# A pair loop of causal attention written in cycles of four steps instead of two, with batch jobs two at a time in every second cycle

## The reference

```python
x = x + attn_a(layernorm(x), ...)      # softmax(q k^T / 4 + bias, causal) v, then Wo
x = x + ffn(layernorm(x), ...)
x = x + attn_b(layernorm(x), ...)      # rotary q, k; the same softmax
x = x + ffn(layernorm(x), ...)
```

## Time and profile before

| what | value |
|---|---|
| median of 3 runs | 4371.92 us (4366.13 to 4383.42) |
| span of the profiled execution | 4403.8 us |
| PE busy | 4131.5 us (94%) |
| DVE busy | 2924.1 us (66%) |
| ACT busy | 2789.4 us (63%) |
| mean granted clock of PE | 0.970 of full |

### The profile page before, as it was taken

The page is one execution under the profiler, slowest core; times in us unless marked ns, Lnnn a source line. Parts: engine busy times, 40 slices in busy tenths (PEclk is TensorE's granted clock), DMA queues, the critical chain, the costliest instruction groups (busy, mean ns, idle before and its releaser), DMA issues.

```text
span 4403.8 us, 107634 instructions
## 1 busy us (share of the span) xinstructions
PE 4131.5 (94%) x42369; PEld 2542.9 (58%) x42369; DVE 2924.1 (66%) x3987; ACT 2789.4 (63%) x5907; POOL 816.1 (19%) x832
## 2 busy tenths in 40 slices
PE   5799999999999999998989999999999999998875
PEld 4455555555555555557855555555556555554764
DVE  3777787778776887771057778777887688773000
ACT  2377777777777776673247777777777777666211
POOL 3010001110121023410013330333023310110012
PEclk9799999999999999999989999999999999999988
DMA  5223223422333333335533432333333322221553
GB/s 168 46 70 75 51 51 81 106 75 53 86 84 84 71 97 102 100 80 174 179 85 97 121 93 51 106 103 98 63 98 95 97 68 59 61 67 50 165 170 117
DMA packets 247473, 407.02 MB, mean 92 GB/s; under 512 B 29324, under 2 KB 162188, under 8 KB 233868
## 3 DMA queue, kind: packets, MB, share of 16 engines
q1 hardware_dynamic: 243896, 391.76, 33.4%
q0 software_dynamic: 3072, 8.39, 0.6%
HBM read 264.25 MB, written 121.50 MB: 88 GB/s over the span
## 4 chain that ended last, share of the span: by engine, by line
PE 81%; DVE 5%; ACT 4%; issue 4%; DMA 3%; SPq 1%; POOL 1%; another core or an unknown queue 0%; ACTq 0%; POOLq 0%; DVEq 0%
PE ps_acc L874 23%; PE ps_r L817 22%; PE ps_p L842 11%; PE ps_r L911 5%; PE ps_r L958 5%; PE ps_p L947 4%; DVE part_max L1074 4%; ACT probs L710 4%; PE ps_r L915 3%; PE ps_r L825 3%; PE ps_r L919 2%; PE ps_p L850 1%; DMA hid_f<-rows_by_expert 1%; PE ps_r L905 1%; PE ps_r L922 1%
## 5 line engine op out<-in xcount | busy, mean ns | idle before, releaser
L1074 DVE TENSOR_REDUCE part_max<-ps_p 128x2 f32<-128x1024 f32 (+3 forms) x2560 | 2599.6, 1060 | 806.6 <-PE ps_p L842 489.0
L710 ACT ACTIVATE probs<-ps_r 128x512 f32<-128x512 f32 (+1 forms) x4608 | 2291.7, 578 | 458.3 <-PE ps_r L817 199.7
L817 PE MATMUL ps_r<-q_stack,k_stack 54*128 54x512 f32 (+3 forms) x5120 | 1647.9, 440 | 61.0 <-issue 16.5
L842 PE MATMUL ps_p<-k_stack,q_stack 52*128 52x512 f32 (+3 forms) x5120 | 1150.8, 407 | 56.9 <-DVE part_max L1074 31.7
L817 PEld LDWEIGHTS ps_r<-q_stack,k_stack 54*128 54x128 f32 x5120 | 721.8, 186 | 784.2 <-ACT probs L710 524.3
L874 PE MATMUL ps_acc<-probs,v_head 128*17 128x256 f32 x19456 | 1156.7, 362 | 2.4 <-ACT acc_sb L718 1.2
L874 PEld LDWEIGHTS ps_acc<-probs,v_head 128*17 128x17 f32 x19456 | 491.3, 97 | 412.0 <-ACT probs L710 135.5
L842 PEld LDWEIGHTS ps_p<-k_stack,q_stack 52*128 52x128 f32 x5120 | 595.4, 189 | 134.9 <-DVE part_max L1074 95.1
L1150 DVE COPY xf<-ps_r 128x256 f32<-128x256 f32 x60 | 25.5, 425 | 459.2 <-PE ps_r L958 459.2
L825 PE MATMUL ps_r<-id,mk 64*128 64x64 bf16 x4096 | 306.6, 195 | 0.0
L911 PE MATMUL ps_r<-xT,wqkv 128*128 128x256 f32 x1024 | 269.1, 397 | 1.9 <-ACT xT L727 1.9
(11 more groups left out here) (90 smaller groups left out, 2094.8 us busy)
## 6 DMA issues: line engine op xcount, KB each, us to landing
probs<-w_dram SPq DMA_DIRECT2D x60, 1024.0 KB, 8.4
q_stack<-parts SPq DMA_DIRECT2D x384, 128.0 KB
k_stack<-parts SPq DMA_DIRECT2D x384, 128.0 KB
parts<-pa SPq DMA_DIRECT2D x128, 256.0 KB, 2.4
parts<-pb SPq DMA_DIRECT2D x128, 256.0 KB, 3.0
o_sums<-acc_sb SPq DMA_DIRECT2D x1024, 17.0 KB
bk<-o_sums SPq DMA_DIRECT2D x64, 256.0 KB
bk<-recips SPq DMA_DIRECT2D x64, 256.0 KB
```

The costliest lines, as they stand in the source:

```text
L710: act.activation(probs[:, at % PBUF, u, 0:w], block_bank(g, n, u)[:, 0:w], ACT.Exp)\
L817: mm[u] = pe.matmul(block_bank(g, n, u)[:, col:col + QW - q0], ks[s][r, kb * P:(kb + 1) * P], qs[s][r, qt * QW + q0:(qt + 1) * QW], start= ...
L842: mm[u] = pe.matmul(banks[:, u, col:col + w], qs[s][r, qb * P:(qb + 1) * P], ks[s][r, kc * QW:kc * QW + w], start=i == 0, stop=True, skip_ ...
L1074: mm = dve.tensor_reduce(part_max[:, :, qb, kc], ps_p[:, p1_banks(g, n), col:col + w], AX_X, ALU.max)
```

## The change

The loop over two steps becomes a loop over four (`CYCLE = 4`), nine cycles for a pair. In a cycle the four units, the eight single-head blocks of scores, and two slots for `times_v` are placed in a new order, which the rows below show. The ring is ordered accordingly, with the jobs of a cycle behind the first block of scores. The units and scores that follow `times_v` (and, in cycles with jobs, the unit behind the jobs) issue their mask products ahead of their score products. `times_v` of a group goes to the first slot at which its steps are done (`value_slots`).

Batch jobs lie in the first, third, fifth ... cycle of a batch, two in each (`slot_step(k) = 8 * (k // 2)`, 72 slots in a batch of 72 cycles). `xt` now turns two row tiles at once, with four products in place of two and one copy of 512 columns. The `c` transposes go to steps 4 and 28. The reciprocal of the softmax sums is done in two halves.

```diff
+CYCLE = 4
+def value_slots():
+    ready = [CYCLE * c + half for c in range(CYCLES + 1) for half in range(2)]
+    ...
-C_HI, C_LO = 30, 6
-JOB_STEPS = (2, 10, 16, 20, 24, 28, 34)
+C_HI, C_LO = 28, 4
+Y_SLOTS = (8, 13, 18, 23, 28, 33, 38, 43, 48, 57, 59, 61, 66, 68, 69, 70)
+def slot_step(k):
+    return 2 * CYCLE * (k // 2)
...
+            def score(g, n, u, masks_first=False):
...
-                for n in range(0, STEPS, 2):
-                    score(g, n, (0, 1))
-                    if g + 1 < NG:
-                        unit(g + 1, n)
-                    score(g, n + 1, (0,))
-                    if g + 1 < NG:
-                        unit(g + 1, n + 1)
-                    score(g, n + 1, (1,))
-                    if n in GROUP_AT:
-                        times_v(g, GROUP_AT[n])
-                    elif n == 0 and g % (NG // 2):
-                        times_v(g - 1, GROUPS - 1)
+                for n in range(0, STEPS, CYCLE):
+                    turned = any(j[0] in RING_JOBS for j in JOBS[g][n])
+                    unit(g + 1, n)
+                    score(g, n, 0)
                     for j in JOBS[g][n]:
                         job(*j)
+                    unit(g + 1, n + 1, masks_first=turned)
+                    score(g, n, 1)
+                    score(g, n + 1, 0)
+                    unit(g + 1, n + 2)
+                    score(g, n + 1, 1)
+                    value_slot(g, n // 2)
+                    unit(g + 1, n + 3, masks_first=True)
+                    score(g, n + 2, 0)
+                    score(g, n + 2, 1)
+                    score(g, n + 3, 0)
+                    value_slot(g, n // 2 + 1)
+                    score(g, n + 3, 1, masks_first=True)
...
                 if kind == "xt":
                     for k in range(KD):
-                        mm = pe.transpose(to[:, k * P:(k + 1) * P], xl[:, i, k * P:(k + 1) * P], identf[:, :])
+                        for t in range(2):
+                            mm = pe.transpose(to[:, k * D + t * P:k * D + (t + 1) * P],
+                                              xl[:, 2 * i + t, k * P:(k + 1) * P], identf[:, :])
```

More of the change, by code:

```diff
@@ L116, in batch_jobs @@
     r = beta - 1 if beta > 0 else None
-    out, loaded, xt_from = [], 0, 22
-    if r is not None:
[L119 to L137, removed]
+    out = []
@@ new lines, in rows @@
+    def rows(f, c, t):
+        return [(t, ("ld", f, c, 0))] + [(t + 7 + 2 * i, ("ln", f, c, i)) for i in range(len(NORM_FROM))]
+    if beta < 0:
+        out += rows(0, 0, -40)
+    if f is not None:
+        at = [slot_step(k) for k in F_SLOTS]
+        for c in range(NQ):
+            x0, x1, at = at[0], at[1], at[2:]
+            nxt = (f, c + 1) if c + 1 < NQ else (f + 1, 0)
+            if nxt[0] < NB:
+                out += rows(nxt[0], nxt[1], x1 + 2)
+            out += [(x0, ("xt", f, c, 0)), (x1, ("xt", f, c, 1)), (x1 + 3, ("cs", f, c, 0))]
+            for kind, u in TURN[c]:
+                if kind == "v":
+                    out += [(at[0], ("v", f, c, u))]
+                    at = at[1:]
+                else:
+                    q1 = at[1]
+                    out += [(at[0], ("qk", f, c, 2 * u)), (q1, ("qk", f, c, 2 * u + 1)),
+                            (q1 + 2, ("sw", f, c, u)), (q1 + 3, ("sp", f, c, u)), (q1 + 10, ("st", f, c, u))]
+                    at = at[2:]
@@ L142, in batch_jobs @@
[L142 to L145, removed]
-    return out
+                out += [(y_at[i], ("y", r, c, i)), (y_at[i] + 2, ("ba", r, c, i))]
+            if routed(r, c):
+                out += [(done + i, ("fn", r, c, i)) for i in range(len(NORM_FROM))]
+            out += [(done + 1, ("bs", r, c, 0))]
+    return out
@@ L777, in _ @@
             for g in range(NG):
-                for n in range(0, STEPS, 2):
+                for n in range(0, STEPS, CYCLE):
                     exp_block(g, n, 0)
+                    for j in JOBS[g][n]:
+                        job(*j)
                     exp_block(g, n, 1)
@@ L802, in _ @@
             mm.then_inc(bias_mm, 1)
-            def score(g, n, heads):
+            def score(g, n, u, masks_first=False):
                 s = g % SLOTS
@@ L830, in unit @@
-            def unit(g, n):
+                pe.wait_ge(ring_used, PLACE[("s", g, n, u)] - RING + 1)
+                bank = block_bank(g, n, u)
+                r, half = slice(HALF * u, HALF * u + ROWS), slice(HALF * u, HALF * u + HALF)
+                masks = [col + HALF * part for qt, kb, q0, col in STEP[n] if kb >= 4 * qt for part in range(2)]
+                fresh = True
+                for part, lo in enumerate(masks if masks_first else ()):
+                    pe.matmul(bank[:, lo:lo + HALF], mk[half, 2 + part % 2, :], id64[half, :], start=fresh, stop=False,
+                              skip_group_check=True)
+                    fresh = False
@@ new lines, in score @@
+                for qt, kb, q0, col in STEP[n]:
+                    mm = pe.matmul(bank[:, col:col + QW - q0], ks[s][r, kb * P:(kb + 1) * P],
+                                   qs[s][r, qt * QW + q0:(qt + 1) * QW], start=fresh, stop=True,
+                                   skip_group_check=True)
+                    fresh = False
+                for part, lo in enumerate(() if masks_first else masks):
+                    mm = pe.matmul(bank[:, lo:lo + HALF], mk[half, 2 + part % 2, :], id64[half, :], start=False,
+                                   stop=True, skip_group_check=True)
@@ L924, in job, with value_slot @@
                 mm.then_inc(job_mm, 1)
+            def value_slot(g, k):
+                if k in GROUP_AT:
+                    times_v(g, GROUP_AT[k])
+                elif k == 0 and g % (NG // 2):
+                    times_v(g - 1, GROUPS - 1)
             def turn_slots(ly, i):
```

132 lines of the change are left out of this document (69 added, 63 removed).

## The result

The changed kernel takes 4525.41 us (median of 4 runs, 4513.57 to 4527.54), the kernel before beside it 4377.67 (median of 4): a ratio of **1.034 [1.032, 1.036]**, slower by 148 us. The forecast was 4400, with a range that ended at 4480. One fact for reading: the profiled execution of the kernel before (4403.8) was some 30 us longer than its median; the one of the changed kernel (4525.0) is its median. So the traces differ by less (121 us) than the medians (148).

What follows compares the result with a forecast made beforehand. Bound: a loop of unit n, reduction, unit n + 2. Cycles + 166 us, jobs - 152, net + 14; side work 20 makes 34, less a few + 28: 4432 profiled, 4400 median; range 4300 to 4480, own 4385 to 4435.

Steps and rivals of the forecast that it cites:

- The loop through unit n, its reduction and unit n + 2: Plain cycle: both units share a bank pair between two `times_v`, PE stands some 0.8 us; cycle 5.63 against 5.30.
- The sign given for it: Profile would show loads of units waiting for `part_max` by 0.7 to 0.9 us once in each plain cycle.
- The side work on DVE: Normalisation parts of 0.65 us behind units n + 1 and n + 3 partly show: 20 us, bounds 0 and 36.
- Loads of scores no longer wait for the scalar engine: New order puts a `times_v` or a unit's wait between each block and its bank's exponential; no wait for `probs`.
- Steps 24 to 27: Unit 24's eight masks and two reductions lengthen the chain to unit 26 by about 0.45 us; cycle + 0.8.
- The five plain ones: Plain cycles of a pair without jobs: + 0.33 us each, less one hidden `c` (0.22), 1.43 together.
- A cycle with jobs: Two jobs lie where PE would wait: 6.83 us against 7.23; a pair 0.73 cheaper, 0.55 on average.
- the rival with a further wait there: Job cycle: second job's bank or reduction n + 1 comes 0.3 us late, adding 75 us: 4475; chance 0.15.
- The price that I gave to the first product behind a change of tile: First load behind a change of tile to the next product of the same array rows: 0.34 us.
- smaller drains: Rival: entries into `times_v` cost 0.22, both cycles 0.2 us shorter, 115 us less: 4285; chance 0.22.
- hidden side work: Rival: side work's 20 us go and masked cycles cost less, 2.3 for 2.6; no change; chance 0.20.
- PE runs through: Rival: unit n + 2 does not wait, plain cycle 4.8 us, kernel near 4110; chance 0.03.

Runs made afterwards that it cites:

- Experiment 2: Changed kernel with unit n + 2 moved behind the first `times_v`, unit n + 3 later, and masks leading in unit n + 2 instead: 4376.61 us, ratio 1.000.
- Experiment 1: Changed kernel with four products of zeros added to each of two score blocks in 240 cycles without jobs and without a `c`: 4450.71 us, ratio 1.017.
- experiment 9: Changed kernel with the normalisation parts moved behind the first unit of cycles with jobs: 4456.49 us, ratio 1.018.
- experiment 11: Kernel before, two-step order, with the batch-job half of the change and normalisation parts moved into cycles with jobs: 4364.18 us, ratio 0.998.
- 5: Kernel before, two-step order kept, with the batch-job half of the change alone: 4439.16 us, ratio 1.016.
- experiment 12: Changed kernel with the zero products of Experiment 1 and the normalisation parts placed as in experiment 9: 4407.21 us, ratio 1.007.
- experiment 7: The order of Experiment 2 with two products of zeros added to each of two score blocks in cycles without jobs: 4377.3 us, ratio 1.001.
- experiment 10: The order of Experiment 2 with the normalisation parts placed as in experiment 9: 4319.48 us, ratio 0.987 to the kernel before.
- experiment 3: Changed kernel with masks last everywhere, all three `masks_first` set to False: 4576.19 us, ratio 1.045.

## Why the prediction was wrong

- **The loop through unit n, its reduction and unit n + 2** was right in place and size: 5.66 for 5.63, DVE's gap 0.91 for 0.8 to 0.9. Experiment 2 moves it out (with unit n + 3 and the order of its masks) and takes off 149 us, the clock's part included. The sign given for it was half wrong: of the wait, the profile puts 0.21 on units and 0.31 on scores.
- **The step that failed is one that was not there: the clock.** I read a PE busy 94% at nearly full granted clock and costed every product at that speed, also in an order into which I had just put a wait of 0.8 in each plain cycle. In that order TensorE falls to 1.2 GHz 58 times for 266 us, mostly in or behind masked cycles, against 9 times for 78. Experiment 1 prices it at 75 us net of the zeros' own time where I had nothing. None of the rivals had it either.
- **The side work on DVE** was named, with bounds of 0 and 36 us and a value of 20. It measures 69 (experiment 9), and 75 in the old order (experiment 11 against 5). The sum took only the part that shows in DVE's own loop. As estimated above, that part is 25 to 31 of the 69 and so within its bounds; the other 38 to 44 are the clock again: with parts in steps 12 to 15 of even pairs it fell there 12 times, without them never, and the low clock could reach into the jobs of the next cycle (pair 14, steps 16 to 19: 8.16 us at clock 0.87, where the median with the full clock is 6.93). Clock and side work overlap: 75 and 69 alone, 118 together (experiment 12; 113 by the difference to the kernel before). That is nearly all of the 120 by which I missed. That experiment 12, at 4407, stands where I had forecast this kernel, at 4400, is in part luck: the 4400 hold 20 for side work, which experiment 12 does without. It is 35 us over the kernel before, where the sum without side work gives 8; another 8 are the zeros' own time, and some 20 are left for what follows.
- **Loads of scores no longer wait for the scalar engine: wrong.** They wait 240 us, down from 524 on the page of before. In plain cycles it is hidden in the reduction's wait. In steps 12 to 15, with one `times_v` in place of two, it isn't (0.53 at 3822.74). That cycle was estimated at 0.2 longer and is 0.7 longer (5.25 against 4.57), the last at 0.1 shorter and is 0.5 longer (5.36 against 4.86). Steps 24 to 27 were overestimated (0.3 for 0.8). The five plain ones come to 1.3 for 1.43. Over a pair without jobs 3.2 for the 2.6 forecast, with the clock left out: 38 us more over 64 pairs.
- **A cycle with jobs**: 6.65 for 6.83. Over the nine kinds of cycle in experiment 12, two jobs add 1.2 on average by medians, 0.7 less than before; I had 0.55. This better half pays for a good part of the worse estimates above. The ring and the second job's bank were not late: the rival with a further wait there falls.
- **Masks first at nothing**: wrong by 51 us, in the kernel's favour (38 at full clock). The price that I gave to the first product behind a change of tile was right for units (0.34), and too high where masks lead.
- Of the rivals, smaller drains and hidden side work are refuted; "PE runs through" too, but experiment 2 comes near its idea: most of the wait on the pair of banks goes if the unit is moved.

Left open: why experiment 7 gained nothing, and why the clock falls in steps 0 to 3 and 16 to 19 and not in plain cycles with a wait as long. That waits bring it down is shown by filling them (experiment 1) and by moving what makes them (2 and 9), not by following one fall.

## What to carry to other kernels

When a change puts waits into a loop that runs at full granted clock, price them twice: by their own length, and by what the next microseconds would cost at half clock; count the stretches at 1.2 GHz in the trace, since the slices of the page hide them. In a chain product, reduction, product that shares a bank pair, let a long foreign stretch of TensorE work (here `times_v`) fall between the two products, and put side work on VectorE where TensorE has other work to do meanwhile. Here the two together made the new order 52 us faster than the old (experiment 10). A busy share is no cover: look where its gap lies.

## What the hardware showed that was not expected

- The waits ahead of the half-clock stretch shown are short (loads wait 0.53 at 3822.74 and PE stands 0.35 at 3824.85), and by the profile PE is busy 5.59 of 5.81 us in the cycle ahead. TensorE can lose its clock while the profile calls it busy.
- Adding 1920 products of zeros made the kernel 75 us faster (experiment 1), and 960 in an order with few falls of the clock gained nothing (experiment 7).
- Behind a change of tile, a mask's product (64 rows, 64 columns) lets the next load's product start 0.06 later, a unit's (52 rows, 512 columns) 0.34 later (experiment 3).
